# A two-layer token mixer on one core: halves of x made a stripe ahead, first quads in another order, two differences on GpSimd

## The chip, the cores and the metric

The kernel runs on one NeuronCore of a Trainium2 chip. The metric is device time in microseconds (us). Three runs of the kernel before took 2149.94, 2143.61 and 2145.37 us, median 2145.37.

## The reference, cut to what matters

x is (64, 64, 512) fp32: 64 batches of 64 tokens of width 512, so 4096 tokens. Two layers follow one another.

```python
# layer 0 (V = 512, H = 2048, gelu is the erf form)
q, k, v = x @ Wq, x @ Wk, x @ Wv
a = softmax(q @ k.T * V**-0.5) @ v @ Wp + bp          # per batch
cms = gelu(a @ cW1 + cb1) @ cW2 + cb2 + one_hot(target)
mod = gelu(concat(a, cms) @ mW1 + mb1) @ mW2 + mb2
z = clip(x + cms + mod, 0, 1)
# layer 1, weights chosen by the role of each batch (3 roles, width 256)
h = gelu(z @ W_down[role] + b_down[role])
y = z + h @ W_up[role] + b_up[role]
out = layernorm(y) * gamma[role] + beta[role]
```

## The kernel before, in words

**Precision.** Every operand of a matmul on TensorE is held as two fp32r tiles, a high half (ScalarE casts, "hi") and a low half (VectorE subtracts the high one, "lo"). One fp32 product is three matmuls, hi·hi, lo·hi and hi·lo (`mm3`, L1526, L1527, L1528). So each weight or activation tile costs TensorE three passes, ScalarE one cast and VectorE one subtraction.

**Tiles and stripes.** The 4096 tokens are 8 tiles t of 512 tokens, transposed (width over partitions, DC = 4 chunks c). A stripe s (NS = 4) has two tiles: x1/y1 belong to tile 2s and x2 to tile 2s+1. Each stripe goes through three stages.

- *attention(s)*: Wq and Wk are folded into one matrix, Wv and Wp into another. Four query projections (query 0 to 3) for the first tile and four (4 to 7) for the second, then 8 pairs p of 2 x 4 batches' worth of work (m = 8s+p): scores (L1620), softmax (row_max L1199 to L1204, exp L718, inverse L1208, normalise L724), turn_p (a transposition, L1628; its halves are pt_hi_lo, L1217), values (L1640) with xk, x in rows by token, whose halves are made by split_xk (L730, L1212) from xk_st. split_y (L740, L1227, L1232) makes the halves of values, attended1/attended2 multiply them by the second folded matrix.
- *stage_c(s)* (cW1, cW2): 2x2 block products by a 7-product scheme, P1 to P7. A product's right-hand operands are *forms* (blocks and differences of blocks of the activations, 14 of them: `difference` L1143 on VectorE, then the halves in `form`, L684 on ScalarE and L1148 on VectorE). The hidden width goes in NQ = 8 *quads* Q; each gives four blocks C11, C21, C22, C12 of hidden units, that are summed on VectorE (sum_p6 L1090, sum_p7 L1099, block22 L1104, block21 L1109, block12 L1113), put through gelu (L671, L672), split (hidden_lo, L1084) and multiplied by the second-layer weights (halves from split_w2, L648 and L1041). `part` (L1058) adds the results to the running sums on VectorE. copy_p1 (L652) takes P1 from PSUM. The weights of a quad stand in a ring of RING = 6 slots, filled by ScalarE (L614) and VectorE (L1005); weight_sums (L1032 to L1037) forms their block sums.
- *stage_m(s)* (mW1, mW2): the same over twice the depth, with the forms of stage_c's output added. At its end, part writes the last of the modifier sums.

Between stripes, GpSimd (POOL) loads what z needs: zr (z_rest, the first tile's x, L529), zc (z_cms, its cms, L530), and VectorE makes z: rest (L1253), z1_sum (L1259), z1_clip (L1267) for the first tile, z2_sum (L1274), z2_clip (L1278) for the second. POOL stores it (L507). x for the next stripe is loaded raw (x_st, 1 MB a tile, L504) and split (split_x, L609 and L1000); xk likewise (L498, 256 KB each).

After the four stripes layer 1 runs over 34 pairs of batches, sorted by role: load_z, split_z (L853, L856, L1398), down (L1835, which starts with the bias row `brow`), gelu, up, layer norm (its power on POOL, L544), store.

**Order.** All of it is written out by hand, one in-order instruction stream for each of TensorE (PE), VectorE (DVE), ScalarE (ACT), GpSimd (POOL) and SyncE (SP); semaphores (`wait_ge`, `then_inc`) tie them. An instruction that waits holds up all that stands behind it on its engine. `prod[Pk]` counts finished products Pk, `sum_s` the five block sums of a quad, `hlo_s` the halves of hidden blocks, `form_lo` the forms. z's first two parts wait for the last P3 of a stripe (`prod[P3]`, L523), and query(s+1, 0) waits for the last parts of stripe s.

## Time and profile before

| what | value |
|---|---|
| runs | 2149.94, 2143.61, 2145.37 us; median 2145.37 |
| profiled execution | 2150.73 us, its span 2149.1 us |
| mean granted TensorE clock | 0.989 |
| PE busy | 2040.3 us (95%), 9372 instructions |
| PE weight loads | 1681.7 us (78%) |
| DVE busy | 1437.4 us (67%) |
| ACT busy | 968.3 us (45%) |
| POOL busy | 76.7 us (4%) |
| DMA | 171.08 MB, mean 80 GB/s |
| chain that ended last | PE 84%, DVE 9%, ACT 4%, issue 1%, DMA 1% |

The page gives busy time per engine; the 109 us in which PE is not busy are spread over many short waits, so the view that matters is that of PE's waits, by the line that waits and the line that ended the wait, and then the order of time around each. In rows by time, the first two numbers are the start in us and the busy time in us; `x4` are four instructions run together; `[1.47 <-DVE w_lo L1041]` is the idle time before it and what ended it. PEclk is the granted share of TensorE's full clock.

### The profile page before, as it was taken

What the parts mean: (1) busy time and instruction counts of PE and PEld (TensorE: products, weight loads), DVE (VectorE), ACT (ScalarE), POOL (GpSimd) and SP (SyncE); (2) the same over time, 40 slices, a digit from 0 to 9 for tenths busy, and PEclk for the clock granted to TensorE, in tenths of its full rate; (3) what the DMA queues carried; (4) which work ended last, traced back from release to release, by engine and by line L of the source; (5) the groups of instructions that cost most, each with busy time, mean ns of one, the idle gap of its engine ahead of it and who ended that gap; (6) DMA issues with size and microseconds to landing.
All of it is one profiled execution on the core that took longest, in us unless ns stands there. A gap on an engine that the chain in (4) does not pass through costs nothing.

```text
span 2149.1 us, 28677 instructions
## 1 busy us (share of the span) xinstructions
PE 2040.3 (95%) x9372; PEld 1681.7 (78%) x9373; DVE 1437.4 (67%) x2701; ACT 968.3 (45%) x1953; POOL 76.7 (4%) x144
## 2 busy tenths in 40 slices
PE   7899999999899999999899999999899999999797
PEld 6778878887778878887678878887678878887676
DVE  6777676555776676556776776556776785554887
ACT  4654443333554443333554453333654453333564
POOL 0000000000000000000000000000000000000122
PEclk9999999999999999999999999999999999999999
DMA  4111131113211132114211231114211222112544
GB/s 168 50 50 59 57 111 59 59 53 134 88 50 58 51 118 59 57 32 157 89 50 44 65 118 59 34 55 157 89 40 50 69 96 64 47 59 104 186 126 114
DMA packets 107966, 171.08 MB, mean 80 GB/s; under 512 B 11645, under 2 KB 71552, under 8 KB 104256
## 3 DMA queue, kind: packets, MB, share of 16 engines
q1 hardware_dynamic: 98672, 126.19, 18.6%
q0 software_dynamic: 9168, 43.26, 6.0%
q8 instruction: 72, 1.18, 0.2%
q14 instruction: 54, 0.44, 0.1%
HBM read 141.62 MB, written 27.79 MB: 79 GB/s over the span
## 4 chain that ended last, share of the span: by engine, by line
PE 84%; DVE 9%; ACT 4%; issue 1%; DMA 1%; SPq 0%; DVEq 0%; POOL 0%; ACTq 0%; POOLq 0%
PE y L1526 17%; PE y L1528 17%; PE y L1527 17%; PE x L1526 10%; PE x L1528 10%; PE x L1527 10%; ACT p_exp L718 1%; DVE s_sb L1199 1%; DVE w_lo L1005 1%; DVE a_forms L1148 1%; PE x L1856 1%; DVE f L1143 1%; DVE t_hi_lo L1238 1%; DMA h_tile<-wp 1%; DVE y_hi_lo L1227 0%
## 5 line engine op out<-in xcount | busy, mean ns | idle before, releaser
L614 ACT CAST w_hi<-w_blocks 128x512 fp32r<-128x512 f32 (+1 forms) x476 | 236.5, 515 | 138.7 <-PE y L1528 85.3
L1005 DVE TENSOR_TENSOR w_lo<-w_blocks,w_hi 128x512 fp32r<-128x512 f32 (+1 forms) x476 | 254.7, 559 | 66.3 <-ACT w_hi L614 66.3
L1526 PE MATMUL x<-h_hi,w_hi 128*128 128x512 f32 x512 | 199.6, 390 | 5.9 <-DVE w_lo L1041 5.9
L1526 PE MATMUL y<-h_hi,w_hi 128*128 128x512 f32 x512 | 199.5, 390 | 5.9 <-DVE w_lo L1041 5.9
L1528 PE MATMUL x<-h_hi,w_lo 128*128 128x512 f32 x512 | 199.3, 389 | 0.0
L1528 PE MATMUL y<-h_hi,w_lo 128*128 128x512 f32 x512 | 199.3, 389 | 0.0
L1527 PE MATMUL x<-h_lo,w_hi 128*128 128x512 f32 x512 | 199.2, 389 | 0.0
L1527 PE MATMUL y<-h_lo,w_hi 128*128 128x512 f32 x512 | 199.2, 389 | 0.0
L1526 PE MATMUL x<-a_forms,w_hi 128*128 128x512 f32 x448 | 178.2, 398 | 18.5 <-ACT f L672 8.3
L1526 PE MATMUL y<-a_forms,w_hi 128*128 128x512 f32 x448 | 174.7, 390 | 6.7 <-DVE f L1099 6.7
L1084 DVE TENSOR_TENSOR h_lo<-f,h_hi 128x512 fp32r<-128x512 f32 x256 | 171.3, 686 | 12.3 <-ACT f L672 11.9
L1528 PE MATMUL x<-a_forms,w_lo 128*128 128x512 f32 x448 | 176.9, 395 | 0.0
L1527 PE MATMUL x<-a_forms,w_hi 128*128 128x512 f32 x448 | 176.8, 395 | 0.0
L648 ACT CAST w_hi<-w_st 128x512 fp32r<-128x512 f32 x128 | 78.7, 621 | 215.7 <-PE y L1528 118.8
L1527 PE MATMUL y<-a_forms,w_hi 128*128 128x512 f32 x448 | 174.4, 389 | 0.0
L1528 PE MATMUL y<-c_forms,w_lo 128*128 128x512 f32 x448 | 174.3, 389 | 0.0
L1528 PE MATMUL y<-a_forms,w_lo 128*128 128x512 f32 x448 | 174.3, 389 | 0.0
L1526 PE MATMUL y<-c_forms,w_hi 128*128 128x512 f32 x448 | 174.3, 389 | 0.0
L1527 PE MATMUL y<-c_forms,w_hi 128*128 128x512 f32 x448 | 174.3, 389 | 0.0
L1109 DVE TENSOR_TENSOR f<-p_copy,y 128x512 f32<-128x512 f32 x32 | 22.0, 686 | 194.1 <-PE y L1528 194.1
L671 ACT ACTIVATE h_hi<-f,bias_sb 128x512 fp32r<-128x512 f32 x128 | 92.8, 725 | 66.0 <-issue 61.2
L1526 PEld LDWEIGHTS x<-a_forms,w_hi 128*128 128x128 f32 x448 | 85.5, 191 | 41.3 <-issue 23.9
(239 smaller groups left out, 4230.9 us busy)
## 6 DMA issues: line engine op xcount, KB each, us to landing
w_blocks<-w1m SPq DMA_DIRECT2D x128, 256.0 KB, 3.4
w_blocks<-w1c SPq DMA_DIRECT2D x64, 256.0 KB, 3.2
w_st<-w2c SPq DMA_DIRECT2D x64, 256.0 KB, 3.2
w_st<-w2m SPq DMA_DIRECT2D x64, 256.0 KB, 3.9
zs<-z_by_batch SPq DMA_DIRECT2D x68, 128.0 KB, 2.1
xk_st<-xk POOLq DMA_DIRECT2D x32, 256.0 KB, 3.0
cms<-f SPq DMA_DIRECT2D x32, 256.0 KB, 2.8
z_cms<-cms POOLq DMA_DIRECT2D x8, 1024.0 KB, 6.5
```

The lines of the kernel that those rows point to most:

```text
L614: nc.scalar.copy(w1_hi[:, w % RING, cols], src).then_inc(w1_hi_s, 1)
L648: nc.scalar.copy(w2_hi[:, j, :], w2_st[:, j, :]).then_inc(w2_hi_s, 1)
L671: nc.scalar.activation(hidden_dst(which)[0], src, ACT.Gelu, bias=bias)
L718: ins = nc.scalar.activation(pe_[r, r], s_sb[r, :], ACT.Exp, bias=nmx[r, :], scale=SCALE, accum_out=rs[r, :])
L1005: nc.vector.tensor_tensor(w1_lo[:, w % RING, cols], src, f32(w1_hi[:, w % RING, cols]), ALU.subtract).then_inc(w1_lo_s, 1)
L1084: nc.vector.tensor_tensor(lo, half_f32(gi), f32(hi), ALU.subtract).then_inc(hlo_s, 1)
L1109: nc.vector.tensor_tensor(f1[:, 1, :], pc[:, Q % 2, :], GB[Q // NQ % 2][2][:], ALU.add).then_inc(sum_s, 1)
L1143: nc.vector.tensor_tensor(out_, in0, in1, ALU.subtract).then_inc(diff_s, 1)
L1148: nc.vector.tensor_tensor(tile[:, i, 1, :], place(i), f32(tile[:, i, 0, :]), ALU.subtract).then_inc(form_lo, 1)
L1526: nc.tensor.matmul(ps, w[0], x[0], start=first, stop=False, skip_group_check=more)
L1527: nc.tensor.matmul(ps, w[0], x[1], start=False, stop=False, skip_group_check=more)
L1528: return nc.tensor.matmul(ps, w[1], x[0], start=False, stop=last, skip_group_check=more)
```

## The change

It does this, part by part:

- (a) **Halves a stripe ahead.** In stage_m of stripes 0 to 2, POOL brings each of 16 pieces of next stripe's x and xk (256 KB) into pre_x; ACT and DVE split it (`split_pre`, two in each quad); POOL stores both halves to DRAM (`pass_x`), and takes the next piece when they are stored. Attention then loads ready halves (2 MB a tile of x, 512 KB an xk). split_x and split_xk stay for stripe 0 alone.
- (b) **z's loads.** zr and zc wait for `prod[P2]` in place of `prod[P3]`, but stand behind the last piece's stores. x's halves come behind them.
- (c) **First quads.** P2 is taken in halves between P5, P7, P6, P4 before the others of its forms; sum_p6 and sum_p7 stand between forms; the first block's gelu works in another buffer (pc). `RHS` becomes a table for each stage.
- (d) **Two of eight differences on GpSimd**, those of P4 (`last_difference`).
- (e) **split_w2(Q, 0)** of a stage's last quad is moved ahead of its parts.
- (f) **Attention's order.** Query 4 is split round scores(0), queries 5 to 7 are whole; scores(4) comes before values(3); split_y comes before the softmax or inverse of the next pair; attended1(0) is split round turn_p(4).
- (g) **Start.** rows_hi, rows_lo and the six brow DMAs go to the end; sort_gather comes after query 2 and sort_pairs, on DVE, after query 3 of stripe 0.
- (h) **End.** W_up gets a staging tile of its own (up_st); its load no longer waits for W_down's split. split_l1 and split_z are interleaved, and `part` comes before split_z(1).

The diff, cut to its core:

```diff
-RHS = {P1: (0, 2), P2: (1, 3), P3: (4, 8), P5: (5, 9), P7: (6, 10), P6: (7, 11), P4: (12, 13)}
+RHS = ({P1: (0, 2), P2: (1, 3), P3: (4, 9), P5: (5, 10), P7: (6, 11), P6: (7, 12), P4: (8, 13)},
+       {P1: (0, 2), P2: (1, 3), P3: (4, 8), P5: (5, 9), P7: (6, 10), P6: (7, 11), P4: (12, 13)})
...
@@ SP @@
-            sp.wait_ge(l1_lo, R)
-            sp.dma_start(l1_st, wu.rearrange("p r k n -> p r (k n)")).then_inc(l1_loaded[1], 16)
...
-            for n in range(4):
+            for n in range(2):
                 load_z(n, n)
+            sp.dma_start(up_st[:], wu.rearrange("p r k n -> p r (k n)")).then_inc(l1_loaded[1], 16)
+            for n in range(2, 4):
+                load_z(n, n)
+            sp.wait_ge(row_lo, 1)
+            sp.wait_ge(brow_zero, 1)
...
@@ POOL @@
+            def pass_x(b):
...
+                if b:
+                    pool.wait_ge(pre_stored, 32 * b)
+                pool.dma_start(pre_x[:], xk[m] if by_token else xT[t, :, c, :]).then_inc(pre_in, 16)
+                pool.wait_ge(pre_lo_s, b + 1)
+                dst = xk_dram[m] if by_token else x_dram[t, :, :, c, :]
+                pool.dma_start(dst[0], f32(pre_hi[:])).then_inc(pre_stored, 16)
+                pool.dma_start(dst[1], pre_x[:]).then_inc(pre_stored, 16)
...
+            def last_difference(g, h):
...
+                nc.gpsimd.tensor_tensor(f1[:, h + 2, :], f1[:, h + 2, :], f2[:, h + 2, :], ALU.subtract).then_inc(t4_s, 1)
...
+                for g in (2 * s, 2 * s + 1):
+                    for h in range(2):
+                        last_difference(g, h)
                 pool.wait_ge(form_lo, 2 * NF * (s + 1))
                 pool.dma_start(f2[:], xT[2 * s + 1]).then_inc(x2_in, 16)
-                pool.wait_ge(prod[P3], 2 * NQ * (s + 1))
                 if s + 1 < NS:
-                    load_x(2 * s + 2)
+                    for b in range(4 * NP):
+                        pass_x(4 * NP * s + b)
+                    pool.wait_ge(pre_stored, 32 * 4 * NP * (s + 1))
...
+                pool.wait_ge(prod[P2], 2 * NQ * (s + 1))
                 pool.dma_start(zr[:], xT[2 * s]).then_inc(zr_in, 16)
                 pool.dma_start(zc[:], cf_dram[2 * s]).then_inc(zc_in, 16)
+                pool.wait_ge(prod[P3], 2 * NQ * (s + 1))
                 if s + 1 < NS:
-                    load_xk(2 * NP * (s + 1))
-                    load_xk(2 * NP * (s + 1) + 1)
-                    load_x(2 * s + 3)
+                    load_x_halves(2 * s + 2)
+                    load_x_halves(2 * s + 3)
+                    load_xk_halves(2 * NP * (s + 1))
+                    load_xk_halves(2 * NP * (s + 1) + 1)
...
@@ DVE, quad(Q) @@
                 split_next(Q, 4)
                 split_next(Q, 5)
+                if Q // NQ % 2 and Q < 2 * NQ * (NS - 1):
+                    split_pre(pre + 1)
+                if q == NQ - 1:
+                    split_w2(Q, 0)
                 if q:
                     for i in range(3):
                         part(Q - 1, i)
...
@@ DVE, attention(s) @@
                     split_pt(m)
-                    if p + 1 < 2 * NP and p not in (NP - 1, NP):
-                        inverse(m + 1)
                     if p and p != NP:
                         split_y(m - 1)
-                    if 0 < p < NP:
-                        query(s, DC + p)
+                    if p == NP - 1:
+                        row_max(m + 1)
+                    if p + 1 < 2 * NP and p != NP:
+                        inverse(m + 1)
+                    if p < NP - 1:
+                        query(s, DC + p + 1)
                     if p in (NP - 1, 2 * NP - 1):
                         split_y(m)
...
@@ PE, attention(s) @@
+                query(s, DC, (0, 1))
                 scores(m0)
-                query(s, DC)
+                query(s, DC, (2, 3))
                 scores(m0 + 1)
...
@@ DVE, after the stripes @@
             split_l1(0)
+            split_z(0, 0)
...
+            split_l1(1)
             for i in range(DC):
                 part(Q, i)
+            split_z(1, 1)
             for c in range(DC):
                 rest(s, c)
-            split_l1(1)
-            for n in range(2):
-                split_z(n, n)
```

Three places in the order. In these rows, `xN` is N instructions run together and the shape is that of the result.

**POOL at a stripe's end.** Before (f<-xT loads x into f2 once stage_m's forms stand; x_st and xk_st are raw x, z_rest and z_cms are zr and zc):

```order
L522 DMA f<-xT 128x2048
L504 DMA x_st<-xT 128x2048
L529 DMA z_rest<-xT 128x2048
L530 DMA z_cms<-cms 128x2048
L498 DMA xk_st<-xk 128x512 x2
L504 DMA x_st<-xT 128x2048
```

and now, from the last of the 16 pieces on:

```order
L523 DMA pre_x<-xk 128x512
L526 DMA xk_halves<-pre_hi 128x512
L527 DMA xk_halves<-pre_x 128x512
L568 DMA z_rest<-xT 128x2048
L569 DMA z_cms<-cms 128x2048
L512 DMA x_hi_lo<-x_halves 128x2x2048 x2
L509 DMA xk_hi_lo<-xk_halves 128x2x512 x2
```

The loads of z_rest and z_cms stood behind a load of 1 MB. They stand behind a load of 256 KB, its split on two engines and two stores; x's loads, now of 2 MB each, follow them.

**DVE in attention, from pair 3's split_y to pair 4's inverse.** Before (L1227 and L1232 are split_y(3), L1199 to L1204 row_max(4), L1208 the inverse, which waits for ScalarE's exp):

```order
L1227 TENSOR_TENSOR y_hi_lo<-x,y_hi_lo 128x2x128
L1227 TENSOR_TENSOR y_hi_lo<-y,y_hi_lo 128x2x128
L1232 TENSOR_TENSOR y_hi_lo<-x,y_hi_lo 128x2x128
L1232 TENSOR_TENSOR y_hi_lo<-y,y_hi_lo 128x2x128
L1199 TENSOR_REDUCE s_sb<-x 64x64 x2
L1202 TENSOR_REDUCE mx<-s_sb 128x1
L1204 TENSOR_SCALAR nmx<-mx 128x1
L1208 RECIPROCAL rinv<-rs 128x1
```

and now (L1303 and L1306 are split_y, L1269 to L1274 row_max, L1278 the inverse):

```order
L1269 TENSOR_REDUCE s_sb<-x 64x64 x2
L1272 TENSOR_REDUCE mx<-s_sb 128x1
L1274 TENSOR_SCALAR nmx<-mx 128x1
L1278 RECIPROCAL rinv<-rs 128x1
L1303 TENSOR_TENSOR y_hi_lo<-x,y_hi_lo 128x2x128
L1306 TENSOR_TENSOR y_hi_lo<-x,y_hi_lo 128x2x128
L1303 TENSOR_TENSOR y_hi_lo<-y,y_hi_lo 128x2x128
L1306 TENSOR_TENSOR y_hi_lo<-y,y_hi_lo 128x2x128
```

Pair 4's maxima and inverse stood behind all four parts of split_y(3); they stand ahead of them.

**DVE in the first quad of stage_m.** Before (L1090, L1099, L1104 are sum_p6, sum_p7, block22; L1032 to L1037 weight_sums; L1005 the ring; L1109 block21; L1084 hidden_lo; L1113 block12):

```order
L1090 TENSOR_TENSOR p_copy<-p_copy,y 128x512
L1099 TENSOR_TENSOR f<-p_copy,y 128x512
L1104 TENSOR_TENSOR f<-f,y 128x512
L1005 TENSOR_TENSOR w_lo<-w_blocks,w_hi 128x512
L1032 TENSOR_TENSOR w_blocks<-w_blocks 128x512
L1033 TENSOR_TENSOR w_blocks<-w_blocks 128x512
L1035 TENSOR_TENSOR w_blocks<-w_blocks 128x512
L1037 TENSOR_TENSOR w_blocks<-w_blocks 128x512
L1005 TENSOR_TENSOR w_lo<-w_blocks,w_hi 128x512 x3
L1109 TENSOR_TENSOR f<-p_copy,y 128x512
```

and now (in the same order L1160, L1169, L1174; L1102 to L1107; L1075; L1179):

```order
L1160 TENSOR_TENSOR p_copy<-p_copy,y 128x512
L1169 TENSOR_TENSOR f<-p_copy,y 128x512
L1213 TENSOR_TENSOR c_forms<-f,c_forms 128x512 x2
L1174 TENSOR_TENSOR f<-f,y 128x512
L1102 TENSOR_TENSOR w_blocks<-w_blocks 128x512
L1103 TENSOR_TENSOR w_blocks<-w_blocks 128x512
L1105 TENSOR_TENSOR w_blocks<-w_blocks 128x512
L1107 TENSOR_TENSOR w_blocks<-w_blocks 128x512
L1075 TENSOR_TENSOR w_lo<-w_blocks,w_hi 128x512 x3
L1289 TENSOR_TENSOR pre_x<-pre_x,pre_hi 128x512
L1179 TENSOR_TENSOR f<-p_copy,y 128x512
```

sum_p6 and sum_p7 stand ahead of the last two forms, P3's ring slot ahead of both, and split_pre (L1289), which waits for a load, ahead of block21 and so of all that comes behind it, block12 among it.

## Rows read from the trace of the kernel before

In a timeline the columns are start and busy time in us, engine, line, operation, result and operands, shapes, count, and in brackets the idle time before it and what ended that.

**Rows 1.** PE's waits: engine, tile, line, what ended them: us in total, times, longest

```profile
PE y L1640 <- DVE pt_hi_lo L1217: 10.8, 11, 2.3
PE x L1526 <- ACT f L672: 8.3, 4, 2.1
PE y L1835 <- DVE z_lo L1398: 8.1, 1, 8.1
...
PE y L1526 <- DVE f L1099: 6.7, 4, 1.7
...
PE x L1620 <- DVE t_hi_lo L1238: 6.6, 8, 1.4
PE y L1526 <- DVE w_lo L1041: 5.9, 4, 1.5
...
PE x L1526 <- ACT p_copy L652: 3.6, 4, 0.9
```

**Rows 2.** Timeline of POOL, DVE and PE from stripe 0 to stripe 1

```profile
506.92 0.53 POOL L529 DMA_DIRECT2D z_rest<-xT  x1 [0.24 <-issue]
507.10 1.29 DVE L1005 TENSOR_TENSOR w_lo<-w_blocks,w_hi 128x512 fp32r<-128x512 f32 x2
...
517.52 2.49 DVE L1253 TENSOR_TENSOR z_rest<-z_rest,z_cms 128x512 f32<-128x512 f32 x4
519.93 2.72 DVE L1259 SCALAR_TENSOR_TENSOR z_rest<-x,bias_sb,z_rest 128x512 f32<-128x512 f32 x4
522.56 2.47 DVE L1058 TENSOR_TENSOR f<-y,f 128x512 f32<-128x512 f32 x4
523.77 0.39 PE L1526 MATMUL y<-x_hi_lo,w_hi 128*128 128x512 f32 x1
```

**Rows 3.** DMA issues from 500 to 530 us: KB each, median us to landing

```profile
x_st<-xT POOLq DMA_DIRECT2D x2, 1024.0 KB, 5.1
...
z_rest<-xT POOLq DMA_DIRECT2D x1, 1024.0 KB, 6.9
```

**Rows 4.** DMA issues of the whole span, same columns

```profile
cms<-f SPq DMA_DIRECT2D x32, 256.0 KB, 2.8
z_cms<-cms POOLq DMA_DIRECT2D x8, 1024.0 KB, 6.5
```

**Rows 5.** Timeline of attention in stripe 1, DVE, PE and ACT round pair 4

```profile
561.41 0.59 DVE L1199 TENSOR_REDUCE s_sb<-x 64x64 f32<-64x128 f32 x2
562.14 0.39 PE L1526 MATMUL y<-y_hi_lo,w_hi 128*128 128x512 f32 x1
563.60 0.40 ACT L724 ACTIVATE p_norm<-p_exp,rinv 128x128 f32<-128x128 f32 x1 [0.23 <-DVE rinv L1208]
```

**Rows 6.** Timeline of stage_m's first quads in stripe 1, POOL, DVE and PE

```profile
782.45 0.55 POOL L522 DMA_DIRECT2D f<-xT  x1 [205.05 <-DVE c_forms L1148]
...
790.98 0.68 DVE L1113 TENSOR_TENSOR p_copy<-p_copy,y 128x512 f32<-128x512 f32 x1
791.87 0.40 PE L1526 MATMUL y<-a_forms,w_hi 128*128 128x512 f32 x1
```

**Rows 7.** POOL's lines: count, busy us, mean ns, idle before

```profile
L544 POOL TENSOR_TENSOR rstd<-veps,mhalf 128x1 f32<-128x1 f32 x34 | 19.6, 577 | 38.3 <-DVE veps L1455 38.2
```

**Rows 8.** Windows: us, busy PE, PEld, DVE, ACT, POOL, then PEclk, DMA, GB/s

```profile
512.00:518.00 6.00, 5.24 (x23) 4.37 (x24) 5.41 (x10) 4.54 (x8) 0.11 (x1) 1.00 0.84 348
...
612.00:616.00 4.00, 4.00 (x12) 2.87 (x11) 3.20 (x7) 4.00 (x10) 0.00 (x0) 0.57 0.17 49
...
1996.00:2000.00 4.00, 3.44 (x15) 3.15 (x16) 2.01 (x3) 2.84 (x9) 0.00 (x0) 0.50 1.01 393
```

**Rows 9.** Windows of DVE alone at the start: rows_hi/rows_lo, then the sort

```profile
22.00:22.80 0.80, 0.77 (x4) 1.00 0.62 251
38.10:40.60 2.50, 2.22 (x13) 0.50 0.76 284
```

**Rows 10.** Timeline of PE, the first instruction of down

```profile
1996.09 0.58 PE L1835 MATMUL y<-brow,ones 128*128 x1 [8.05 <-DVE z_lo L1398]
```

More of the change, by code:

```diff
@@ L144, in program @@
             pick = sb("pick", [1, 3, NPAIR], on=sorting)
-            rows_f = sb("rows_f", [R, KD], on=sorting)
-            rows_hi, rows_lo = hl("rows", [R, KD], sorting)
         with ExitStack() as l1_small:
@@ L190, in program @@
             z_hi, z_lo = hl("z", [P, 2, DC, P], at_l1)
+            brow = sb("brow", [P, R, KD], F32R, at_l1)
+            rows_f = sb("rows_f", [R, KD], on=at_l1)
+            rows_hi, rows_lo = hl("rows", [R, KD], at_l1)
         with ExitStack() as at_cf:
@@ L335, in _ @@
             sp.dma_start(tgt_i[:], target.to_broadcast([P, B])).then_inc(const_in, 16)
-            sp.wait_ge(row_lo, 1)
-            sp.wait_ge(brow_zero, 1)
-            for r in range(R):
-                sp.dma_start(f32(brow[0:1, r, :]), f32(rows_hi[r:r + 1, :])).then_inc(row_in, 16)
-                sp.dma_start(f32(brow[1:2, r, :]), f32(rows_lo[r:r + 1, :])).then_inc(row_in, 16)
             sp.wait_ge(wa_out, DC)
@@ L683, in form @@
                     act.wait_ge(c1_s, DC * s + i + 1)
-                nc.scalar.copy(forms[g % 2][:, i, 0, :], place(i)).then_inc(form_hi, 1)
+                nc.scalar.copy(forms[g % 2][:, i, 0, :], place(g, i)).then_inc(form_hi, 1)
             def quad(Q):
@@ L1175, in quad @@
                 split_next(Q, 2)
+                if Q // NQ % 2 and Q < 2 * NQ * (NS - 1):
+                    split_pre(pre)
                 block21(Q)
@@ L1188, in tail @@
                 part(Q - 1, 3)
-                for j in range(2):
-                    split_w2(Q, j)
+                split_w2(Q, 1)
                 hidden_lo(Q, C22)
@@ L1428, in _ @@
                     for c in range(DC):
-                        split_x(2 * s + 2, c)
-                    for c in range(DC):
                         rest(s, c)
@@ L1653, in attention @@
                     turn_p(m)
-                    for c, k in query2_step(p):
-                        query(s, DC + c, (k,))
+                    if p < NP - 1:
+                        query(s, DC + p + 1)
+                    else:
+                        scores(m0 + NP)
                     if p + 2 < NP:
```

373 lines of the change are left out of this document (215 added, 158 removed).

## The prediction, made before the changed kernel ran

> **What bounds the kernel now.** The page comes first: TensorE is busy 2040.3 of 2149.1 us (95%) and is 84% of the chain, so only PE's idle time (109 us) and its clock can be won. The next view is the list of PE's waits [rows 1]. The reader is to see that none is large and that they repeat by stripe: four waits for the gelu of a first quad in cW1 (8.3 us), four for sum_p7 in cW1 and in mW1 (each 1.7), four for P1's copy (0.9), the tails of stages (w_lo L1041, 1.5 each time), scores(0) and its like (6.6 over 8), values behind the softmax (10.8 over 11), and one of 8.1 before layer 1. Last come the timelines round four of these places, the windows for the clock, and the order of the instructions. A wait is worth its length only if nothing else ends just behind it.
>
> **The sum**, against the profiled execution (2150.7 us; the median of the runs is 2145.4, so 5.3 less).
>
> *Start (g).* The four rows of rows_hi/rows_lo leave DVE's chain before the first query: 0.77 us [rows 9], taken at -0.7. The sort's chain, 2.22 us for 13 instructions [rows 9], comes in ahead of row_max(0), where scores wait for DVE. **+2** for stripe 0's attention, between 0 (covered by query 4) and 2.5.
>
> *Attention, stripes 1 to 3 (f, a).* scores(0) behind half a query wins most of its 1.4 us [rows 1], and splits of x and xk leave DVE and ACT. Against that, DVE takes row_max(4), waits for the exp, and inverts before split_y(3). Now row_max(4) starts at 561.41 and the normalise that follows the inverse at 563.60; attended1(0), which needs split_y(3), starts at 562.14 without a wait [rows 5]. So split_y(3) moves by some 2.2 us plus its own place, and attended1(0) comes 2 to 3 us late, unless scores(4), now ahead of values(3), fills it. I put gain and loss equal, **0** a stripe, between -3 and +2.
>
> *First quad of cW1 (c, d).* P1's copy, the gelu and sum_p7 come earlier: of the 0.9, 1.7 and 2.1 us [rows 1] some 0.9 net would go, since the next quad's P5 and P1 then wait in turn for block sums and ring slots. The two differences on GpSimd have no row. The nearest is a 128x1 operation, 577 ns each [rows 7]: that is the lower bound for 128x512; 0.68 us, what DVE takes for a like one [rows 6], is the next, and three times that, 2.1, the upper. I take 1.1. Whether DVE is held while GpSimd runs no row shows: the bounds are 0 and the whole 1.1 each, 2 in a stage, and I take half, 0.55, about the DVE time that each saves. So **-0.3** each, -1.2 in all, between -3.6 (no hold) and +1.4.
>
> The Trainium skill, "SBUF — State Buffer", section "Who interferes with whom", says that a VectorE instruction with two SBUF inputs and a GpSimd instruction that reads SBUF exclude each other for their whole length; no row of before shows two such at once. By it the four terms here would be +1.4 and not -1.2.
>
> *Stage tails (e).* split_w2(Q, 0) no longer stands behind three parts, so the 1.5 us [rows 1] at the end of cW1 go: **-6**. At mW1's end it counts for the last stripe alone, **-1.5**; in the others the next stripe's start waits for something later (below).
>
> *First quad of mW1 (c, a, d).* Here today's order is just in time: block12 ends at 791.66 and P5 of the next quad starts at 791.87, without a wait [rows 6]. sum_p7's wait (1.7) goes, P4 starts 1.4 earlier. But split_pre now stands before block21 and block12. Its piece cannot be asked for before f<-xT, 1 MB, which POOL issues at 782.45 [rows 6] (about 1 us later with the new forms); 1 MB took 5.1 us [rows 3], and the piece lands behind it, at some 789.4 to 791.6. Then come a cast and a subtraction, block21, two halves and a ring slot, and block12. I get P5 1.7 us later than today without a hold of DVE and 3.6 with a full one: **+2.6** for each of three stripes. In the last there is no piece: +0.6. Together +8.4, between +4.7 and +12.4.
>
> *Stripe boundary (a, b).* Now zr is issued at 506.92, right after the last P3; zr takes 6.9 us to land behind x_st [rows 2, 3], rest starts at 517.52, z1_sum at 519.93, the parts at 522.56, and query 0 at 523.77 [rows 2]. In the change the last split_pre stands behind the last ring slots, whose halves DVE makes from 507.10 for 1.29 us [rows 2]; so it ends near 509.0. Two stores of 256 KB (2.8 us, rows of SP's like ones [rows 4], the second issued half a us after the first) land near 512.7. Only then is zr issued, at 512.8, 5.9 us later than today, though it waits for P2 and no longer for P3. It lands 5.1 later [rows 3], 517.9, and zc, the next MB, 2.5 behind it, 520.4. DVE then needs rest 2.49, z1_sum 2.72 and one part of 0.62 [rows 2]: 526.3 for query 0. **+2.5** three times, +7.5. x's halves (2 MB) land at 525.5 by the same rate, so it is z and not x that ends last, but only just.
>
> The clock comes on top. After the wait of 1.5 us at the tail it stayed 1.00 (512 to 518); after one of 2.1 it was 0.57 (612 to 616), after one of 8.1 it was 0.50 (1996 to 2000) [rows 8, 1, 10]. The tail now ends near 522.1 at the latest and the engine waits for over 4 us, where today waits at this place are short. At 0.5 for some 5 us half the work is lost: **+2.4** three times, +7.2, bounds 0 and +10.
>
> *End (h).* down(0) starts at 1996.09 after 8.05 us [rows 10]. W_up's halves no longer wait for W_down's split and lie before the parts; these stand where the z halves did. By DVE's order the last part ends near 1990, brow's rows have landed at 1989.4: **-6**, between -4.5 and -7.5.
>
> Sum: -0.7 + 2 + 0 - 1.2 - 6 - 1.5 + 8.4 + 7.5 + 7.2 - 6 = **+9.7**, so 2160.4 for a profiled execution and **2155.0** against the median. Nothing else is charged: the stores and pieces add 36 MB on queues that are 80 GB/s full on the mean, in stage_m, where no wait for a DMA is listed [rows 1].
>
> **The rivals.**
>
> 1. *DVE is held by GpSimd for the whole length.* Against: no row. For: only the order, that differences for P4 stand beside DVE's forms. It gives +1.4 for -1.2 and +12.4 for +8.4, with late forms for P4 behind: +6.6 to +14 on the sum, 2162 to 2169. No row bears it out or speaks against it: **0.20**. (The section of the Trainium skill named above, "SBUF — State Buffer", would make this the case.)
>
> 2. *Attention gains more.* If scores(4) ahead of values(3) covers the late split_y(3), values(4) (1.7 of [rows 1]'s 10.8) and scores(0) gain 3 to 4 us a stripe: -12 on the sum, 2143, no change. For it: ScalarE and DVE lose 8 casts and 8 subtractions of xk and x a stripe. Against: DVE's in-order wait for the exp. **0.16**.
>
> 3. *The boundary is covered: faster.* The one place is zc's landing. If zr and zc come in by 516, that is if the last split_pre ends before 505 (ring slots free earlier) or the transfers go at the rate of 6.5 us for the last of two [rows 4] without x_st ahead, then rest starts 1.5 us before today's 517.52, as DVE has no split_x left, query 0 starts at 522, and neither the 7.5 nor the 7.2 is paid: -1.7 three times for them. The sum is then -10 and, with attention's gain, -20: 2136 to 2126. It decides at a zc that lands before 517.5. Against: the order of POOL, which puts it behind the stores. **0.16**.
>
> The forecast itself has 0.48, with a range of its own of 2147 to 2163 (the bounds of mW1's first quad, the clock and attention). That the change does nothing at all can't be: each moved row is in the order.
>
> **How the numbers follow.** About 0.3% (6.4 us) is what a measurement of this kernel can tell from no change. Faster by more is rival 3, 0.16, and a little of rival 2: 0.17. Slower by more: most of the forecast (0.40 of 0.48; its lower edge is within 6.4 us), nearly all of rival 1 (0.18 of 0.20): 0.58. The rest, 0.25, is no change. The range leaves out about 0.2: the faster half of rival 3 and the outer end of rival 1 with the clock's upper bound: 2136 to 2172.
>
> **What the profile after would show.** The list of PE's waits: no w_lo of split_w2 at 1.5; sum_p7 gone in mW1; a new wait of over 4 us, three times, before query 0 with a part behind it; P5 of the second mW1 quad waiting for block12; the wait before down at about 2. The timeline of the boundary: zr issued behind the stores at about 6 us after the last P3, PEclk near 0.5 after it. In attention, attended1(0) waiting for split_y(3) by 2 to 3 us. GpSimd's subtraction at 1.1 us, DVE's rows beside it longer by half of that. The prediction is wrong if zr's issue is not behind the last stores, if PE's clock stays at 1.00 after the boundary, or if attention from query 0 to attended2 is shorter by 3 us than before, or longer by as much.

## The result, and the profile after

The changed kernel takes 2171.28 us (median of 4 runs, 2168.32 to 2173.38) against 2144.61 for the kernel before: a ratio of 1.0118, 95% interval 1.0096 to 1.0141, so 25 us slower by the ratio, 27 by the medians. Slower was forecast, and 2171.3 lies inside 2136 to 2172, but the forecast was 2155.0, a loss of 9.7 us: the measured one is over two and a half times as large. The profiled execution has a span of 2171.5 us, 22.4 more than the one before.

The page of the changed kernel, its first part and its clock:

```profile
PE 2065.0 (95%) x9372; PEld 1699.7 (78%) x9373; DVE 1442.9 (66%) x2685; ACT 965.1 (44%) x1953; POOL 197.0 (9%) x304
...
PEclk9899999999999999999899999999899999999998
```

The same 9372 matmuls keep TensorE busy 24.7 us longer (2040.3 before), while the time in which it is not busy fell from 108.8 to 106.5 us. So none of the 22.4 us is waiting on balance: 4.6 us more stand behind PE's last matmul, 6.9 fewer ahead of it. What grew is the time that the matmuls themselves take, at the lower clock: the mean granted clock went from 0.989 to 0.976. Adding up (1 - PEclk) over windows of 5 us, the time "lost at half clock" from here on, gives 24.8 us before and 53.2 now. Most stretches at half clock lose 1.7 us each.

PE's waits in the changed kernel (engine, tile, line, what ended them: us in total, times, longest), where [rows 1] stood:

```profile
PE y L1604 <- DVE f L1128: 13.0, 3, 4.8
PE x L1604 <- ACT p_copy L711: 8.2, 4, 2.0
PE y L1604 <- DVE p_copy L1183: 7.9, 4, 2.6
...
PE x L1706 <- ACT p_norm L793: 6.9, 12, 0.6
PE y L1604 <- DVE y_hi_lo L1306: 6.6, 4, 1.9
...
PE y L1930 <- DVE z_lo L1475: 4.9, 1, 4.9
PE x L1604 <- DVE p_copy L1183: 4.9, 4, 1.2
PE x L1604 <- DVE f L1169: 3.9, 4, 1.0
```

The first row is new: three waits of over 4 us before query 0 (f L1128 is the last parts). The second, P2 in cW1's first quad behind P1's copy, has grown from 3.6 us to 8.2. The third is block12 (L1183), for which P5 of mW1's second quad waits, the fifth split_y(3) before attended1(0). Gone are the tails' waits for w_lo, most of sum_p7's, the gelu's, and 3.1 of 8.1 us before down.

By stage, from the timelines (each from its first matmul to the next stage's), in us:

| stage | before | after | change | forecast |
|---|---|---|---|---|
| start to query 0 | 36.34 | 34.82 | -1.5 | -0.7 |
| attention, stripe 0 | 72.35 | 78.79 | +6.4 | +2 |
| attention, stripes 1 to 3 | 72.25, 73.26, 73.24 | 74.99, 76.07, 76.30 | +8.6 | +7.2, all clock from the boundary |
| cW1, 4 stripes | 688.15 | 674.75 | -13.4 | -7.2 |
| mW1, stripes 0 to 2, with the wait for query 0 | 729.22 | 750.86 | +21.6 | +15.3 |
| mW1, stripe 3, with the wait for down | 251.28 | 246.81 | -4.5 | -6.9 |
| layer 1, to PE's last matmul | 142.80 | 143.31 | +0.5 | 0 |
| behind it, to the end of the span | 10.2 | 14.8 | +4.6 | 0 |

**The boundary**, stripe 0 to 1, timeline of DVE, POOL and PE in the changed kernel ([rows 2] before):

```profile
512.01 0.69 DVE L1183 TENSOR_TENSOR p_copy<-p_copy,y 128x512 f32<-128x512 f32 x1 [0.83 <-PE y L1606]
...
514.42 0.69 DVE L1289 TENSOR_TENSOR pre_x<-pre_x,pre_hi 128x512 fp32r<-128x512 f32 x1
...
518.87 0.54 POOL L568 DMA_DIRECT2D z_rest<-xT  x1 [2.40 <-DMA xk_halves<-pre_x]
...
527.36 2.50 DVE L1327 TENSOR_TENSOR z_rest<-z_rest,z_cms 128x512 f32<-128x512 f32 x4 [6.04 <-DMA z_cms<-cms]
...
533.14 0.80 PE L1604 MATMUL y<-x_hi_lo,w_hi 128*128 128x512 f32 x1 [4.85 <-DVE f L1128]
```

The last P3 ends at 512.0 (block12, L1183, starts on it). The last split_pre ends 3.1 us behind it and zr is issued 6.9 us behind it, in the order that the forecast had, each 1 us later than it had put them (2.1 and 5.9). rest starts 8.5 us after that issue, where 7.6 was forecast. The first query matmul takes 0.80 us where [rows 2] have 0.39.

**Windows** of the changed kernel (columns as in [rows 8]), behind the boundary and at pairs 3 and 4 of stripe 1:

```profile
533.00:538.00 5.00, 4.86 (x12) 3.89 (x13) 1.88 (x4) 0.00 (x0) 0.00 (x0) 0.52 1.02 410
570.00:580.00 10.00, 8.12 (x37) 6.95 (x36) 6.17 (x21) 3.99 (x15) 0.72 (x1) 0.73 0.48 157
```

**Attention**, PE's timeline in stripe 1, one row where each of turn_p(3), scores(4), values(3), scores(5) and attended1(0) begins:

```profile
566.88 0.33 PE L1706 MATMUL x<-ident,p_norm 128*128 128x128 f32 x1 [0.62 <-ACT p_norm L793]
...
568.08 0.39 PE L1698 MATMUL x<-x_hi_lo,t_hi_lo 128*128 128x256 f32 x1 [0.87 <-DVE t_hi_lo L1312]
...
569.59 0.41 PE L1721 MATMUL x<-pt_hi_lo,xk_hi_lo 128*128 128x256 f32 x1
...
571.19 0.52 PE L1698 MATMUL x<-x_hi_lo,t_hi_lo 128*128 128x256 f32 x1
...
574.55 0.47 PE L1604 MATMUL y<-y_hi_lo,w_hi 128*128 128x512 f32 x1 [1.88 <-DVE y_hi_lo L1306]
```

From 564.5 to 574.5 PE has no matmul of 512 columns, only short ones and four waits. Before, three quarters of query 7 stood in that place. The clock falls to half inside it, from 568.5 to 571.9 us, and again from 575.4 to 578.8 and from 592.4 to 595.8. The kernel before has one such stretch in this stage.

**mW1's first quads.** P5 of the second quad waits 2.45 us in stripe 0 (its row stands with e4 below), and a half-clock stretch follows it, in stripes 1 and 2 too. The windows behind it in stripes 0 and 1:

```profile
309.00:313.00 4.00, 4.00 (x12) 3.10 (x12) 1.48 (x3) 0.40 (x1) 0.54 (x1) 0.57 0.35 99
804.00:808.00 4.00, 4.00 (x12) 3.09 (x12) 1.19 (x2) 0.12 (x1) 0.54 (x1) 0.57 0.36 102
```

**GpSimd's differences**, the group of POOL's lines, then single rows of POOL and of DVE beside them:

```profile
L540 POOL TENSOR_TENSOR f<-f 128x512 f32<-128x512 f32 x16 | 37.8, 2363 | 765.5 <-DVE f L1208 765.5
```

```profile
112.40 1.60 POOL L540 TENSOR_TENSOR f<-f 128x512 f32<-128x512 f32 x1 [23.33 <-DVE f L1208]
112.76 1.52 DVE L1075 TENSOR_TENSOR w_lo<-w_blocks,w_hi 128x256 fp32r<-128x256 f32 x1
...
287.80 4.00 POOL L540 TENSOR_TENSOR f<-f 128x512 f32<-128x512 f32 x1 [165.94 <-DVE f L1208]
...
290.71 1.63 DVE L1213 TENSOR_TENSOR c_forms<-f,c_forms 128x512 fp32r<-128x512 f32 x1
```

A 128x512 subtraction takes 1.6 us at best, 2.36 on the mean of the 16 (with what it waits for DVE) and 4.0 at worst; the same on DVE takes 0.69. DVE's 128x256 subtraction beside it took 1.52, its 128x512 one 1.63. The next 128x256 one, at 115.41, took 0.41. Where DVE's operations follow one another closely, as from 287.5 to 290.6 us, it is GpSimd that waits (4.00). That is the exclusion which the Trainium skill, "SBUF — State Buffer", section "Who interferes with whom", states for a VectorE instruction with two SBUF inputs; these rows agree, in both directions.

### The profile page after: what moved, and what is told of

Its sections match the earlier page's. It is cut to its first block, busy times and chain, and to the rows that moved or that the text cites. A ratio compares the mean times of both kernels' runs of the same rounds, so it can differ in the third digit from the quotient of the medians.

```text
span 2171.5 us, 28816 instructions
## 1 busy us (share of the span) xinstructions
PE 2065.0 (95%) x9372; PEld 1699.7 (78%) x9373; DVE 1442.9 (66%) x2685; ACT 965.1 (44%) x1953; POOL 197.0 (9%) x304
## 3 DMA queue, kind: packets, MB, share of 16 engines
q0 software_dynamic: 22992, 93.60, 12.3%
## 4 chain that ended last, share of the span: by engine, by line
PE 73%; DVE 13%; SPq 4%; issue 4%; DMA 3%; ACT 3%; POOL 0%; DVEq 0%; ACTq 0%; POOLq 0%
PE y L1604 15%; PE y L1606 15%; PE y L1605 15%; PE x L1604 9%; PE x L1606 9%; PE x L1605 9%; DVE w_lo L1075 1%; SPq L417 1%; DMA z_cms<-cms 1%; SPq L418 1%; DVE a_forms L1213 1%; DVE c_forms L1213 1%; DMA pre_x<-xT 1%; DVE s_sb L1269 1%; DVE f L1208 1%
## 5 line engine op out<-in xcount | busy, mean ns | idle before, releaser
L1075 DVE TENSOR_TENSOR w_lo<-w_blocks,w_hi 128x512 fp32r<-128x512 f32 (+1 forms) x476 | 259.7, 570 | 63.2 <-ACT w_hi L671 62.9
L1604 PE MATMUL x<-a_forms,w_hi 128*128 128x512 f32 x448 | 175.8, 393 | 17.5 <-ACT p_copy L711 8.2
L1605 PE MATMUL x<-a_forms,w_hi 128*128 128x512 f32 x448 | 174.3, 389 | 0.0
L1154 DVE TENSOR_TENSOR h_lo<-f,h_hi 128x512 fp32r<-128x512 f32 x248 | 166.0, 687 | 10.8 <-ACT f L731 10.8
L705 ACT CAST w_hi<-w_st 128x512 fp32r<-128x512 f32 x128 | 78.7, 621 | 204.1 <-PE y L1606 107.0
L1179 DVE TENSOR_TENSOR f<-p_copy,y 128x512 f32<-128x512 f32 x32 | 22.0, 687 | 183.7 <-PE y L1606 183.7
## 6 DMA issues: line engine op xcount, KB each, us to landing
xk_hi_lo<-xk_halves POOLq DMA_DIRECT2D x24, 512.0 KB, 4.1
```

What stands on the lines that cost most here:

```text
L705: nc.scalar.copy(w2_hi[:, j, :], w2_st[:, j, :]).then_inc(w2_hi_s, 1)
L1075: nc.vector.tensor_tensor(w1_lo[:, w % RING, cols], src, f32(w1_hi[:, w % RING, cols]), ALU.subtract).then_inc(w1_lo_s, 1)
L1154: nc.vector.tensor_tensor(lo, half_f32(gi), f32(hi), ALU.subtract).then_inc(hlo_s, 1)
L1179: nc.vector.tensor_tensor(f1[:, 1, :], pc[:, Q % 2, :], GB[Q // NQ % 2][2][:], ALU.add).then_inc(sum_s, 1)
L1604: nc.tensor.matmul(ps, w[0], x[0], start=first, stop=False, skip_group_check=more)
L1605: nc.tensor.matmul(ps, w[0], x[1], start=False, stop=False, skip_group_check=more)
```

## The experiments

My theory after the profile: four separate places lose time, each by a wait, or by a thin stretch (short matmuls with waits between them), together with the half clock behind it: the boundary, attention's order, mW1's first quad, GpSimd. The rivals stand in each expectation. In the first four runs one place each is taken out of the changed kernel; the kernel before took 2144.73 us beside them, and gains on the changed kernel are differences of such medians or ratios.

Each kernel has one profile. In places whose code is the same, profiles differ too: stripe 0's attention takes 78.7 to 80.0 us in the changed kernel, e1, e2 and e4, and e1 has a stretch of half clock in stripe 0's cW1 that the changed kernel lacks. So a stage's difference under 2 us is to be trusted only where it repeats over stripes.

### e1: the boundary

```diff
@@ POOL @@
-                    pool.wait_ge(pre_stored, 32 * 4 * NP * (s + 1))
...
                 if s + 1 < NS:
+                    pool.wait_ge(pre_stored, 32 * 4 * NP * (s + 1))
                     load_x_halves(2 * s + 2)
@@ ACT and DVE, quad(Q), behind split_next(Q, 3); the old place keeps q < NQ - 1 @@
+                if Q // NQ % 2 and Q < 2 * NQ * (NS - 1) and q == NQ - 1:
+                    split_pre(pre + 1)
```

> The changed kernel with its stripe boundary altered alone: in the last quad of stage_m the last piece is split right after ring slot 3, in DVE's idle time before block12, and the wait for the last stores stands behind zr's and zc's loads, ahead of x's halves. Theory (z ends last at the boundary, and the idle time drops the clock): in the profile of the change zr is issued 6.9 us after the last P3 and query 0 waits 4.85, 4.05 and 4.12 us, after which some 3.4 us are lost at half clock. With zr issued about 1.5 us after the last P3, rest starts near 521 instead of 527.4, the wait before query 0 is under 1.5 us, PEclk stays at 1.00 behind it, and the whole gets 15 to 22 us shorter. Rival (x's own halves, 2 MB that take 14.0 us to land, end just as late): they move only by the 3.2 us of the earlier split, the wait stays at 2 us or more, the clock still falls, and the gain is 3 to 9 us. Second rival (the clock falls there whatever the wait is): wait gone, PEclk after it still near 0.6, gain 8 to 12 us.

2152.93 us, ratio 1.0036 (1.0024 to 1.0049): 18 us less than the changed kernel. zr is issued at 513.35, rest starts at 522.18, PE's waits list no wait before query 0, and the windows from 528 to 538 us keep the clock:

```profile
528.00:533.00 5.00, 5.00 (x24) 4.12 (x23) 2.73 (x5) 0.59 (x1) 0.00 (x0) 1.00 0.99 402
533.00:538.00 5.00, 5.00 (x24) 4.14 (x23) 1.84 (x4) 1.18 (x2) 0.00 (x0) 1.00 0.64 258
```

The theory holds, both rivals fall: x's halves land in time, and the clock falls for the idle time.

### e2: GpSimd

```diff
-                nc.gpsimd.tensor_tensor(f1[:, h + 2, :], f1[:, h + 2, :], f2[:, h + 2, :], ALU.subtract).then_inc(t4_s, 1)
+                nc.vector.tensor_tensor(f1[:, h + 2, :], f1[:, h + 2, :], f2[:, h + 2, :], ALU.subtract).then_inc(t4_s, 1)
```

(with its waits on DVE, after the forms that it depends on).

> The changed kernel with P4's two differences made by DVE again, 16 in all, beside nothing else changed. Theory (GpSimd and DVE shut each other out): on GpSimd one takes 1.58 us at best, 4.00 at worst, and DVE operations beside it take 1.1 us longer; so on DVE it costs 0.69 us each, no DVE operation in the forms is stretched, and the first quads get no longer: 2 to 8 us shorter in all, most of it in stage_m's first quads. Rival (off DVE is a gain, since DVE paces the forms): the first quads wait 0.5 to 0.7 us longer each, 4 to 6 us slower. No difference beyond 2 us would mean that the forms have slack and GpSimd's part decided nothing.

2160.45 us, ratio 1.0071 (1.0055 to 1.0088): 10 us less, more than the 2 to 8 expected. The rival (slower by 4 to 6) falls. In the profile cW1 is 0.5 to 0.8 us a stripe shorter, mW1 1.3 to 2.7. The direction holds; run e11 below measures it again.

### e3: attention's order

```diff
@@ PE @@
-                query(s, DC, (0, 1))
                 scores(m0)
-                query(s, DC, (2, 3))
+                query(s, DC)
...
-                    if p < NP - 1:
-                        query(s, DC + p + 1)
-                    else:
-                        scores(m0 + NP)
+                    for c, k in query2_step(p):
+                        query(s, DC + c, (k,))
...
                     values(m)
+                scores(m0 + NP)
                 scores(m0 + NP + 1)
```

(and ACT's and DVE's order, and split_y, as in the kernel before).

> The changed kernel with attention's order of before on all three engines (and split_y as before); ready halves of x and xk stay. Theory (the new order costs stripe 0 its 6.4 us and is even in the others): query 4 no longer waits 2.65 us for the last split of x in stripe 0, and scores(4), values(3), scores(5) no longer stand in one stretch of short matmuls ahead of a wait for split_y(3); stripe 0's attention takes 72 to 74 us and not 78.8, the clock lost between 565 and 600 us falls from some 3.9 us to 1.7, and the waits of attention grow from 5.6 to 8 or so. Total 4 to 9 us shorter. Rival (the new order is a gain once stripe 0 is left out): stripes 1 to 3 get 2 to 3 us longer each and the total stays within 3 us. Second rival (the clock in attention falls because of the idle time at the boundary before): the loss at half clock behind pair 3 stays as it is, 3 to 5 us a stripe.

2162.16 us, ratio 1.0085 (1.0067 to 1.0103): 7 us less by the ratios, whose intervals overlap a little, 9 by the medians. The stages tell more: stripe 0's attention 72.80 us (78.79 in the changed kernel), stripes 1 to 3 72.86, 73.08, 73.11 (74.99 to 76.30), with 2.0 to 2.4 us more of waits in each and 3.4 to 5.5 us less lost at half clock. So the new order costs 2.1 to 3.2 us in stripes 1 to 3 as well, and both rivals fall. These are upper values: the two profiled executions differ by 15 us, the medians by 9. Part of it comes back: the half clock of 1.7 us in cW1's first quad, absent from the changed kernel, is there again in three of four.

### e4: the first piece

```diff
@@ POOL @@
+                if s + 1 < NS:
+                    pass_x(4 * NP * s)
                 for h in range(2):
                     last_difference(2 * s + 1, h)
@@ ACT and DVE, quad(Q) @@
-                if Q // NQ % 2 and Q < 2 * NQ * (NS - 1):
+                if Q // NQ % 2 and q and Q < 2 * NQ * (NS - 1):
                     split_pre(pre)
...
+                if Q // NQ % 2 == 0 and q == NQ - 1 and Q < 2 * NQ * (NS - 1):
+                    split_pre(4 * NP * (Q // (2 * NQ)))
```

> The changed kernel with the first piece of each stripe passed in stage_c's last quad, so that no split_pre stands ahead of block21 in stage_m's first quad. Theory (the piece's load behind the 1 MB load holds DVE, and through block12 the second quad's P5): the wait of 2.45 us there falls below 0.5 and the 1.7 us lost at half clock behind it go too, stage_m takes 4 us less in stripes 0 to 2: 8 to 13 us shorter in all. Rival (block12 is late for the forms and for GpSimd's differences): the wait stays above 1.5 us, as P4 and sum_p6 set it, and the gain is under 4 us.

2161.23 us, ratio 1.0072 (1.0054 to 1.0091): 10 us less, as expected. The changed kernel's timeline shows what went, the piece's load, its split, block12, and P5 of the second quad:

```profile
299.84 0.54 POOL L523 DMA_DIRECT2D pre_x<-xT  x1
304.92 0.62 ACT L806 CAST pre_hi<-pre_x 128x512 fp32r<-128x512 f32 x1 [2.96 <-DMA pre_x<-xT]
...
307.98 0.68 DVE L1183 TENSOR_TENSOR p_copy<-p_copy,y 128x512 f32<-128x512 f32 x1
...
308.81 0.50 PE L1604 MATMUL y<-a_forms,w_hi 128*128 128x512 f32 x1 [2.45 <-DVE p_copy L1183]
```

In e4 the waits within stage_m are 1.2, 2.4 and 1.2 us in stripes 0 to 2 (3.5, 3.6 and 3.6 in the changed kernel), and stage_m takes 247.79, 247.63 and 246.18 us (750.86 in all before the edit, 741.60 with it). P5 waits 0.2 to 0.3 us for block12 in stripes 0 and 1, and the half-clock stretch behind it is gone in all three stripes.

### e5 to e8: together, and the parts of the change alone

e5_four makes the four edits at once. e6_four_att2 is e5 with most of attention's new order. e7 is the kernel before with one move:

```diff
@@ DVE, quad(Q) @@
                 split_next(Q, 5)
+                if q == NQ - 1:
+                    split_w2(Q, 0)
                 if q:
                     for i in range(3):
                         part(Q - 1, i)
@@ DVE, tail(Q) @@
-                for j in range(2):
-                    split_w2(Q, j)
+                split_w2(Q, 1)
```

and e8 is the changed kernel without parts (a), (d) and (f), with z's loads at P2 and ahead of x's. The kernel before took 2146.72 us beside these.

> The four edits of the first runs together: z's loads early and the last piece split early, P4's differences on DVE, attention's order of before, the first piece in stage_c. Theory (they are separate losses): the gains of 18.4, 10.8, 9.1 and 10.1 us add up to 48, so 2123 us, some 21 us faster than the kernel before; stripe 0's attention near 72.5 us, cW1 near 168.2, mW1 near 241, no wait over 2 us at a stripe boundary. Rival (the half clock is not tied to one place and comes back elsewhere, as attention's old order brought 1.7 us of it back in three of four first quads of cW1): 5 to 12 us of the 48 are lost again, 2128 to 2135. Rival 2 (they overlap, the boundary sets them all): no faster than 2140.

> As the run before, but with most of attention's new order: query 4 round scores(0) in stripes 1 to 3, queries 5 to 7 whole, split_y first; only scores(4) stands behind values(3) again, pair 4's softmax behind split_y(3), and stripe 0's query 4 behind scores(0). Theory (the one move that costs is pair 4's, which puts scores, values and scores ahead of a wait for split_y(3)): the clock falls at most once in attention, attended1(0) starts without a wait, and scores(0)'s 1.4 us are saved: 2 to 5 us a stripe less than with the old order in stripes 1 to 3, 0 in stripe 0, so 6 to 12 us faster than e5_four. Rival (whole queries leave the rest of attention too thin, so the clock falls at pairs 3 and 4 all the same): same as e5_four within 3 us, or slower.

> The kernel before, with only the move of split_w2(Q, 0) ahead of the last quad's parts. Theory (the tails' 1.5 us are DVE's order alone): the wait for w_lo goes at all eight tails; at cW1's four and mW1's last it shortens the whole, at mW1's other three the next stripe's query 0 waits for z instead: 6 to 8 us faster. Rival (the parts behind it are late for the next product's bank): under 3 us. If the boundaries gain too, 10 to 12.

> The changed kernel with parts (a) and (b) undone (raw x and xk loaded and split in attention as before, no pieces; z's loads at P2 and ahead of x's), P4's differences on DVE and attention's order of before. Left of the change: the first quads' order, split_w2, start and end. Theory (making halves ahead gains nothing, since attention is not paced by those splits): within 3 us of e5_four, 2120 to 2130. Rival (ready halves do relieve DVE at the boundary and in attention): 6 to 12 us slower than e5_four, with query 0 waiting 1.5 to 2 us for parts behind split_x, rest and z1_sum. In stage_m it should be 2 us shorter where pieces no longer stand between DVE's steps.

| run | median us | ratio to before | interval |
|---|---|---|---|
| e5_four | 2120.22 | 0.9880 | 0.9865 to 0.9895 |
| e6_four_att2 | 2130.03 | 0.9923 | 0.9910 to 0.9937 |
| e7_before_w2 | 2138.43 | 0.9957 | 0.9943 to 0.9971 |
| e8_raw_x | 2125.47 | 0.9901 | 0.9886 to 0.9916 |

*e5*: the four losses add up; all 51 us between it and the changed kernel are theirs (48 by the sum of the single medians), and nothing of them comes back. In its profile 16 us are lost at half clock (53.2 in the changed kernel). It is the fastest kernel here, with e9 within the noise of it, 26 us faster than the one before. At its boundary rest starts on zc without much of a wait, and query 0 follows the tail at once:

```profile
512.87 2.50 DVE L1344 TENSOR_TENSOR z_rest<-z_rest,z_cms 128x512 f32<-128x512 f32 x4 [0.90 <-DMA z_cms<-cms]
...
518.89 0.47 PE L1626 MATMUL y<-x_hi_lo,w_hi 128*128 128x512 f32 x1
```

*e6*: its theory (6 to 12 us faster than e5) fails and its rival holds: 10 us slower. Attention of stripes 1 to 3 waits 1.6 to 2.8 us less than in e5 and still takes 1.6 to 2.0 us more (72.01, 72.54, 72.61 against 70.44, 70.57, 70.69), stripe 0's 5.5 more. So it was not scores(4)'s place alone. The windows of e6 in stripe 1, and under them those of e5 at the same times, whose query 0 starts 3.7 us earlier; in all of stripe 1's attention e6 loses 3.4 us at half clock and e5 nothing:

```profile
555.00:560.00 5.00, 3.61 (x17) 3.61 (x18) 4.52 (x12) 1.45 (x5) 0.72 (x1) 0.64 0.80 240
560.00:565.00 5.00, 5.00 (x21) 4.37 (x21) 3.57 (x13) 1.28 (x5) 0.00 (x0) 0.68 0.49 179
```

```profile
555.00:560.00 5.00, 5.00 (x32) 4.28 (x31) 3.78 (x14) 1.28 (x5) 0.00 (x0) 1.00 0.73 263
560.00:565.00 5.00, 3.29 (x20) 2.86 (x20) 2.52 (x8) 3.16 (x10) 0.71 (x1) 1.00 0.10 23
```

*e7*: the move of one instruction is worth 8 us, as expected. In its profile cW1 is 11.1 us shorter in all: the tails' waits are gone (5.9 us), and so is the half clock in cW1's first quad in three of four stripes, while attention of stripes 1 to 3 loses 1.7 us more at half clock each. *e8*: without ready halves 5 us slower than e5, between the two expectations. Its query 0 waits 1.1 us behind split_x, rest and z1_sum, and 1.7 us more are lost at half clock in attention of stripes 2 and 3. In the profiles it takes 6.5 us more in span, although its end is 4.5 us shorter (7.4 against 11.9 us behind DVE's last instruction, see e12): the ready halves save 11 us in the stages and give 4.5 back at the end. The 2 us that stage_m was to gain without pieces did not come: 725.9 us in stripes 0 to 2 against 723.1, 3.4 of it the waits before query 0.

### e9 to e12

Three runs on e5 and e6, beside a kernel before of 2145.78 us. e9 and e10 differ by one place each:

```diff
@@ e9, PE, attention(s) @@
+                if s:
+                    query(s, DC, (0, 1))
                 scores(m0)
-                query(s, DC)
+                query(s, DC, (2, 3) if s else range(DC))
@@ e10, PE, attention(s), with ACT and DVE to match @@
-                    if p < NP - 1:
-                        query(s, DC + p + 1)
+                    for c, k in query2_step(p):
+                        query(s, DC + c, (k,))
```

> The fastest kernel so far (e5_four, 2120.2 us, attention in the order of before) with one piece of the new order: in stripes 1 to 3 query 4 is taken half before scores(0), half behind. Theory (scores(0)'s wait of 1.4 us for the halves of query 3 is covered): that wait goes in three stripes, each attention 1.0 to 1.4 us shorter, 3 to 4 us in all, 2116 to 2117. Rival (the softmax behind scores(0) starts later, and turn_p(0) waits instead): no gain, 2119 to 2122.

> e6_four_att2 (2130.0 us) with one edit: queries 5 to 7 are taken in pieces again, three quarters of a query in each of pairs 0 to 3, as before. The clock lost in attention there was 6.45, 3.4, 5.1 and 6.8 us, though its waits were 2 us shorter than in e5_four. Theory (with whole queries none is left for pair 3: turn_p(3), values(3), scores(4) and scores(5) stand alone, a stretch of 6 to 8 us of short matmuls and waits, and the clock is halved there): with pieces the loss falls to 0 to 2 us a stripe, stripe 0's attention from 78.4 to 73 us, the whole to 2115 to 2121. Rival (split_y ahead of the next softmax is what opens the gap): within 3 us of 2130.

> e5_four with P4's differences on GpSimd again: the first run of that edit cost 10.8 us, of which the profile gives 0.5 a stripe in cW1 and 1.3 to 2.9 in mW1, about 9 in all, in part at half clock. Theory (GpSimd and DVE hold each other, so a first quad's forms end later): DVE operations beside L540 are 1 to 2 us longer again, mW1 0.7 to 2 us a stripe longer, cW1 0.5: 5 to 9 us slower than e5_four, 2125 to 2129. Rival (the 10.8 us were mostly clock that fell by the neighbourhood of other waits): 1 to 4 us slower.

| run | median us | ratio to before | interval |
|---|---|---|---|
| e9_q4_split | 2121.26 | 0.9888 | 0.9873 to 0.9903 |
| e10_pieces | 2125.61 | 0.9904 | 0.9889 to 0.9919 |
| e11_t4_pool | 2133.93 | 0.9946 | 0.9932 to 0.9959 |

*e9*: a miss, no gain. Its attention waits 0.3 to 1.2 us less, and 1.7 us more are lost at half clock in each of stripes 1 to 3, in stripe 1 at pair 3 (PEclk 0.66 from 560 to 565 us).

*e10*: half right. With pieces of queries in pairs 0 to 3 the time at half clock in attention of stripes 1 to 3 falls from 3.4, 5.1, 6.8 us to 0, 0, 1.7, and these stages from 72.01, 72.54, 72.61 us to 71.19, 71.19, 72.05. The same window as in e6 (both have query 0 at 522.5 us):

```profile
555.00:560.00 5.00, 4.17 (x29) 3.48 (x28) 4.82 (x15) 1.34 (x4) 0.72 (x1) 1.00 0.80 276
```

PE was busy 4.2 us of it, against 3.6 in e6. But stripe 0's attention stays at 77.20 us (78.37 in e6), where 73 was expected, with 9.5 us of waits and 3.4 lost at half clock; what holds it there beyond the waits for p_norm and pt_hi_lo was not separated. So the missing pieces explain the half clock in stripes 1 to 3. What split_y's place ahead of the softmax costs was not measured by itself.

*e11*: GpSimd's part costs 14 us in e5 too (0.9946 against 0.9880), more than the 5 to 9 expected. In the profile cW1 takes 0.5 to 2.0 us more a stripe, mW1 0.6 to 2.5, and attention of stripes 2 and 3, which the edit does not touch, 1.3 and 1.6 more, at half clock.

**e12** is e7 with 48 copies of 256 KB from DRAM to DRAM on POOL's queue:

```diff
@@ POOL @@
+                    for b in range(2 * NQ):
+                        pool.wait_ge(prod[P1], 2 * NQ * s + NQ + b // 2 + 1)
+                        t, c = 2 * (s + 1) + b // 8, b // 2 % 4
+                        pool.dma_start(x_dram[t, b % 2, :, c, :], xT[t, :, c, :]).then_inc(copied, 16)
+                        pool.wait_ge(copied, 16 * (2 * NQ * s + b + 1))
```

> e7_before_w2 (2138.4 us) with 48 more DMAs on POOL's queue, 16 of 256 KB in each stage_m of stripes 0 to 2, that copy x from DRAM to DRAM and that nothing waits for but POOL. What it tells apart: in every kernel with ready halves the span ends 11.8 to 11.9 us after DVE's last instruction, in every kernel without them (the one before, e7, e8) 7.3 to 7.4 us after it. Theory (the end of the program takes longer the more packets POOL's queue has carried: 22992 against 9168): with the copies the tail is clearly over 7.4 us, between 8.5 and 11.9 by their packets, and the whole that much longer. Rival (it comes with something else of the change, as its further semaphores or the use of tiles by DMA): tail 7.3 to 7.4 us, the whole within 2 us of 2138.4.

2139.94 us, ratio 0.9973 (0.9964 to 0.9983) against e7's 0.9957, whose interval overlaps with it: the whole does not settle the matter. The end does: the span ends 10.2 us after DVE's last instruction (7.3 in e7). So what POOL's queue has carried lengthens the end of the program; the law stays open, as 13008 packets give 2.9 us more than 9168 do, and 22992 only 4.6. The copies change the number and bytes of its DMAs too, and nothing here tells these from the packets.

## Why the prediction was right or wrong

**The step that failed is the clock.** The forecast charged it at one place alone, behind the boundary's wait (+2.4 three times, +7.2), and put every other reordering at its waits: "nothing else is charged". The time lost at half clock rose by 28 us and not by 7. By stage it rose by 6 us in stripe 0's attention, 22 in that of stripes 1 to 3 (the boundary's part among them) and 7 in mW1 of stripes 0 to 2, and fell by 7 in cW1. The prediction named attention longer by 3 us as a sign of being wrong, and stripe 0's is longer by 6.4. Term by term:

- **Attention** ("gain and loss equal, **0** a stripe", and +2 for stripe 0): **this term failed.** The waits came out nearly as said: split_y(3) is 1.88 us late for attended1(0) (2 to 3 was put), and attention's waits fell by 2.4 us in stripe 1. What the term left out is the clock inside attention. It was priced from rows in which one long wait had come first; a stretch of short matmuls with waits of 0.3 to 1.9 us between them was followed by half clock as well. e3 shows the new order to cost 6.0 us in stripe 0, where +2 had been put, and 2.1 to 3.2 in the others. There the 0 came out near the truth by luck: it stood for the order and the ready halves together, and the halves give back 1.9 to 3.0 us a stripe (e5 against e8).
- **mW1's first quads** (+8.4): right in its waits, and too small. P5 of the second quad waits 2.45 us for block12, behind the piece whose load stands behind 1 MB. But three of these first quads, with the waits before query 0 and the tails' gain taken out, cost some 13 us and not 7.8, and the rest is the half clock behind P5's wait, 1.7 us each, which the term had at nothing although [rows 8] show 0.57 behind a wait of 2.1 us. e4 recovers 10 us.
- **The boundary** (+7.5 and +7.2 of clock): right in mechanism, by its own steps. PE waited 4.85, 4.05 and 4.12 us. It was a little too small: zr was issued 1.0 us later behind the last P3 than put, z_cms took 0.9 us longer to land than at the rate assumed, and of the 3.4 us lost at half clock each time 2.3, 2.8 and 3.0 lie behind query 0's start, where 2.4 was put. e1 shows the place to be worth 18 us.
- **Tails** (-6 and -1.5): right in the waits, 5.9 us in cW1; e7 alone gives 8.
- **cW1's first quad** (-1.2): right in the waits, which are 1.1 us shorter in all than e7's. The four stages gained 13.4 us with the tails, and nearly all the rest, 1.7 a stage, is the half clock of [rows 8] at 612 us, which is gone. The first quad's order is not shown to be what removed it: e7, which has only the tails' move, has it gone in three of four.
- **GpSimd**: a second failure of size. Its price was taken as 1.1 us (measured 1.6 at best, 2.36 on the mean) and its hold on DVE as half (the rows show it whole, both ways). Rival 1, at 0.20, had the mechanism: it put 6.6 to 14 us on top of a half hold, and e2 and e11 find 10 and 14 for the whole of GpSimd's part against DVE's doing it, a related but not the same quantity.
- **The end** (-6): half. The wait before down fell by 3.1 us; and 4.6 us at the program's end, which no term had, come with POOL's traffic (e12; by what law is open). A drift of layer 1 of 0.5 us is the rest.
- The range held the time, by its width and not by its terms. The rivals 2 and 3 did not occur; e5 shows rival 3's case, a covered boundary, once the order is changed for it. Parts (c), (g) and (h) were not measured one by one; e8 has them with (e) and the early loads of z, and is 21 us faster than the kernel before, 8 of which e7 gives alone.

## What to carry to other kernels

On a kernel that keeps TensorE 95% busy, count a reordering in two currencies, waits and granted clock: spread the long matmuls over the stretches of short ones, even where that costs a microsecond of waits, since a saved wait that leaves a thin stretch is paid back at half clock. When work is moved ahead to fill a quiet stage, look at the last piece and the first: what stands behind them in the queue (here z's loads and a block sum) matters more than the 14 between. Where a kernel's waits are changed, read the clock behind every new wait (here one of 2.45 us), not only behind the longest. Don't hand a SBUF-to-SBUF operation to GpSimd beside a busy VectorE without pricing both engines for its whole length.
